# Another order at the beginning of six selective-scan runs: staggered halves, one ScalarE table, du's second half behind the first scan units

## The reference, cut to what matters

```
dbc = u @ W_xp                     # 64 + 16 + 16 columns
dt  = softplus(dbc[:64] @ W_dt + b_dt)
h_t = exp(dt_t * A) * h_(t-1) + (dt_t * u_t) * B_t
y_t = sum_s h_t[s] * C_t[s] + u_t * D
```

## Time and profile before

| | |
|---|---|
| median of 3 runs | 1971.57 us (1970.94 to 1975.65) |
| profiled execution | 1970.25 us |
| its span in the trace | 1968.5 us |
| TensorE matmul busy | 1868.5 us (95%) |
| VectorE busy | 1602.0 us (81%) |
| ScalarE busy | 1421.5 us (72%) |
| GpSimd busy | 1046.7 us (53%) |
| mean granted TensorE clock | 0.976 |

### The profile page before, as it was taken

How to read it: one execution, slowest core, us unless ns; L and a number is a source line. 1 busy time by engine, 2 the same in 40 slices (tenths; PEclk the granted TensorE clock), 3 DMA queues, 4 the chain that set the end, 5 groups by cost and what they waited for, 6 DMA issues and landing times. The chain is left out here.

```text
span 1968.5 us, 32685 instructions
## 1 busy us (share of the span) xinstructions
PE 1868.5 (95%) x12312; PEld 1344.0 (68%) x12312; DVE 1602.0 (81%) x2125; ACT 1421.5 (72%) x2666; POOL 1046.7 (53%) x603
## 2 busy tenths in 40 slices
PE   6989999999999999989999999989998999999997
PEld 3664899748997599869995799689974323332323
DVE  5665999668997699879995999689977989999742
ACT  3425999378992899699953999699944277777775
POOL 3031699417994299829980599469943500003000
PEclk9989899999999999999999999999999799999999
DMA  5022212102121112101110112021101111111000
GB/s 199 1 92 90 65 55 59 46 15 79 55 60 49 34 55 60 44 22 56 60 39 2 38 60 55 23 65 55 59 19 28 40 39 38 37 36 37 20 23 22
DMA packets 57548, 95.19 MB, mean 48 GB/s; under 512 B 14951, under 2 KB 23559, under 8 KB 55982
## 3 DMA queue, kind: packets, MB, share of 16 engines
q1 hardware_dynamic: 55854, 88.90, 15.2%
q0 software_dynamic: 1536, 4.20, 0.7%
HBM read 73.55 MB, written 6.91 MB: 41 GB/s over the span
## 5 line engine op out<-in xcount | busy, mean ns | idle before, releaser
L973 POOL TENSOR_TENSOR A<-A 128x1024 f32<-128x1024 f32 x384 | 895.8, 2409 | 231.9 <-ACT small L885 191.9
L893 ACT ACTIVATE A<-A,negA 128x512 f32<-128x512 f32 x768 | 549.1, 717 | 30.5 <-DVE A L954 23.7
L954 DVE TENSOR_TENSOR_SCAN A<-A,small,PS 128x512 f32<-128x512 f32 x384 | 453.8, 1257 | 8.2 <-ACT A L893 5.1
L954 DVE TENSOR_TENSOR_SCAN A<-A,PS 128x512 f32<-128x512 f32 x384 | 431.7, 1198 | 21.6 <-PE PS L806 10.9
L831 PE MATMUL PS<-ident,A 128*128 128x128 f32 x3072 | 401.9, 274 | 12.8 <-POOL A L973 9.4
L806 PE MATMUL PS<-A 128*128 128x128 f32 x3072 | 383.6, 276 | 0.3
L806 PEld LDWEIGHTS PS<-A 128*128 128x128 f32 x3072 | 362.4, 192 | 4.5 <-DVE A L954 1.3
L831 PEld LDWEIGHTS PS<-ident,A 128*128 128x128 f32 x3072 | 348.0, 141 | 20.0 <-POOL A L973 12.2
L1730 ACT ACTIVATE A<-PS 128x512 f32<-128x512 f32 x512 | 267.9, 603 | 123.6 <-PE PS L1693 123.4
L1499 DVE TENSOR_REDUCE A<-PS 128x1 f32<-128x512 f32 x512 | 319.7, 681 | 40.0 <-PE PS L1486 38.6
L870 ACT ACTIVATE A<-A,small 128x512 f32<-128x512 f32 x320 | 229.5, 717 | 14.1 <-PE PS L812 14.0
(11 more groups left out here) (194 smaller groups left out, 1837.9 us busy)
## 6 DMA issues: line engine op xcount, KB each, us to landing
A<-scrc SPq DMA_DIRECT2D x192, 256.0 KB, 3.2
A<-A SPq DMA_DIRECT2D x360, 32.0 KB
scr<-A SPq DMA_DIRECT2D x4, 1024.0 KB, 4.9
W<-in_wa SPq DMA_DIRECT2D x2, 1536.0 KB, 9.8
X<-in_x SPq DMA_DIRECT2D x4, 512.0 KB, 5.4
scr<-W SPq DMA_DIRECT2D x128, 1.5 KB
out<-X SPq DMA_DIRECT2D x4, 512.0 KB, 2.9
W<-in_w SPq DMA_DIRECT2D x1, 1984.0 KB, 7.6
```

The costliest lines, as they stand in the source:

```text
L893: e.activation(A_B[i % 4], r.DT[:, dt, ci * 512:(ci + 1) * 512], ACT.Exp, scale=negA[:, r.n, dt * 16 + s:dt * 16 + s + 1]).then_inc(*decay ...
L954: e.tensor_tensor_scan(h, a, u, init, ALU.mult, ALU.add).then_inc(*scanned.up((q, i)))
L973: e.tensor_tensor(h, h, CB[k % 2].unsqueeze(1).broadcast_to([128, 2, 512]), ALU.mult).then_inc(*weighed.up((q, pair)))
```

## The change

- **Halves staggered.** TensorE's order in a beginning becomes: xd of the first half, `more(0)`, dt of the first, xd of the second, `more(1)`, dt of the second, B turned, `more(2)`, du's first half turned, `more(3)`. ScalarE goes through Abs and Exp of the first half, the second's xd copy, `more(1)`, Abs of the second, B, Ln of the first, Exp and Ln of the second. `more` hands out the other work in parts: in runs 2 and 4 part 0 is the last 2 of this direction's 8 z projections and parts 1 to 3 are 1, 3 and 4 of the next direction's; in runs 3 and 5 part 0 is empty and parts 1 to 3 are 1, 3 and 4 of the gates; in runs 0 and 1 parts 0 and 1 are empty and the fused weights stand whole in part 2 on TensorE and in part 3 on ScalarE.
- **VectorE's other work** (`meanwhile`) moves between the two halves' du.
- **One table.** `preload_exp` goes; one `preload_act_table_set("natural_log_exp_and_others")` stands at the beginning. The gates' Silu is replaced by Identity with the bias, and a separate `open_gates_s` takes Silu in place, half by half, behind ScalarE's scan loop.
- **Next xd early.** Runs 3 and 5 get their first half's xd between the last sums of the run before (`early`, behind pair 61 of 64), and its copy behind ScalarE's loop.
- **du's second half later.** Its four turned blocks follow `form_u(3)` to `form_u(6)`; its copies stand at i = 3 and 4 of the loops of ScalarE and VectorE. All first scalings now stand ahead of the copies of the first half. `form_u(i)` for i < 4 waits for the copy of block i alone.

```diff
+        def turn_du_t(e, w, r, p, j):
+            o = take(w, ("dut", r.q, p, j))
+            w.wait_ge(*dve.at(("du", r.q, p)))
+            for m in range(4):
+                t = e.transpose(o[:, m * 128:(m + 1) * 128], DUD[:, p, m, j * 128:(j + 1) * 128], ident[:, :])
+            t.then_inc(*pe.up(("dut", r.q, p, j)))
...
+            if not begun:
+                banks.seek(4)
+                project_xd_t(e, w, r, r.order[0], ready)
+            more(0)
+            banks.seek(5)
+            project_dt_t(e, w, r, r.order[0])
+            project_xd_t(e, w, r, r.order[1], ready)
+            more(1)
+            banks.seek(3)
+            project_dt_t(e, w, r, r.order[1])
...
+            more(2)
+            banks.seek(4)
+            for j in range(4):
+                turn_du_t(e, w, r, 0, j)
+            more(3)
+            banks.seek(0)
...
+            if not begun:
+                copy_xd_s(e, w, r, r.order[0])
+            more(0)
+            e.preload_act_table_set("natural_log_exp_and_others")
+            size(0)
+            decline(0)
+            copy_xd_s(e, w, r, r.order[1])
+            more(1)
+            size(1)
...
+            log(0)
+            decline(1)
+            log(1)
+            more(2)
...
@@ run_t
                 form_u(i + 3)
+                if i < 4:
+                    turn_du_t(e, w, r, 1, i)
...
                 add_up(pair)
+                if pair == PAIRS_N - 3 and early:
+                    early()
...
@@ run_s
+            for j in range(4):
+                if not first_state(r, j)[2]:
+                    scale_du_s(e, w, r, j)
             for j in range(4):
                 if not first_state(r, j)[2]:
                     copy_du_s(e, w, r, 0, j)
-            if after:
-                after()
+            more(3)
+            w.wait_ge(*act.at(("bt", q, r.order[1])))
             for j in range(4):
                 spread_b(1, j)
-            for j in range(2, 4):
-                copy_du_s(e, w, r, 1, j)
             first_half(w, r)
...
                 if i >= 4:
                     decay(i)
+                if i in (3, 4):
+                    copy_du_s(e, w, r, 1, i - 1)
                 if dt % 2 and i >= 5:
                     keep((i - 5) // 2)
...
@@ run_v
+                if i in (3, 4):
+                    copy_du_v(e, w, r, 1, i - 3)
...
+        PARTS = (slice(0, 0), slice(0, 1), slice(1, 4), slice(4, 8))
...
+        def open_gates_s(e, w, b):
+            w.wait_ge(*act.at(("mx", b)))
+            for p, c in enumerate(runs[3 + 2 * b].order):
+                g = MX[:, :, c * 512:(c + 1) * 512]
+                e.activation(g, g, ACT.Silu).then_inc(*act.up(("gate", b, p)))
```

More of the change, by code:

```diff
@@ L656, in inputs_t @@
                 t.then_inc(*pe.up(("bt", q, c)))
[L657 to L667, removed]
@@ L677, in inputs_s, with copy_xd_s, size @@
+            more(3)
+            banks.seek(0)
+        def copy_xd_s(e, w, r, c):
+            w.wait_ge(*pe.at(("xd", r.q, c)))
+            e.activation(XD[0:96, c * 512:(c + 1) * 512], bank(("xd", r.q, c))[0:96, :], ACT.Copy).then_inc(*act.up(("xd", r.q, c)))
+            banks.give(("xd", r.q, c), act.now())
+        def inputs_s(e, w, r, more, begun=False):
+            q = r.q
+            def size(p):
                 for m in range(4):
-                    w.wait_ge(*pe.at(("dt", q, m, c)))
@@ L741, in inputs_v @@
                 e.tensor_tensor(DUD[:, p, :, :], r.DT[:, :, o], r.U[:, :, o], ALU.mult).then_inc(*dve.up(("du", q, p)))
-            if after:
-                after()
-            w.wait_ge(*act.at(("bt", q, r.order[0])))
+                if meanwhile and p == 0:
+                    meanwhile()
+            if late:
+                late()
+            for j in range(4):
+                if first_state(r, j)[2]:
+                    scale_du_v(e, w, r, j)
             for j in range(4):
@@ L747, in inputs_v @@
                     copy_du_v(e, w, r, 0, j)
-            for j in range(2):
-                copy_du_v(e, w, r, 1, j)
         def second_half(w, r):
@@ L899, in run_s @@
                 decay(i)
-            if meanwhile:
-                meanwhile()
+            for j in range(4):
+                if not first_state(r, j)[2]:
+                    scale_du_s(e, w, r, j)
             for j in range(4):
@@ L1197, in norm3_p, with z_jobs, z_t @@
             norm_p(e, w, ("ln3", b), range(b * TB, (b + 1) * TB))
-        def z_t(e, w, b, n):
+        PARTS = (slice(0, 0), slice(0, 1), slice(1, 4), slice(4, 8))
+        def z_jobs(n):
+            return [(m, c) for c in runs[2 + n].order for m in range(4)]
+        def z_t(e, w, b, n, jobs):
             w.wait_ge(*act.at(("wzc", n)))
-            for c in runs[2 + n].order:
-                for m in range(4):
-                    w.wait_ge(*act.at((("xs", b), c, 1)))
-                    project_t(e, w, ("z2", b, n, m, c), lambda k, m: Wzc[n][:, k, m * 128:(m + 1) * 128], 2, m, lambda k: XS[:, k, c * 512:(c + 1) * 512])
@@ L1206, in z_s @@
-        def z_s(e, w, b, n, halves=(0, 1)):
-            w.wait_ge(*dve.at(("bzc", n)))
-            for c in [runs[2 + n].order[p] for p in halves]:
-                for m in range(4):
-                    w.wait_ge(*pe.at(("z2", b, n, m, c)))
-                    e.activation(Z2[n][:, m, c * 512:(c + 1) * 512], bank(("z2", b, n, m, c)), ACT.Identity,
-                                 bias=Bzc[:, 4 * n + m:4 * n + m + 1]).then_inc(*act.up(("z2", b, n, c)))
-                    banks.give(("z2", b, n, m, c), act.now())
```

142 lines of the change are left out of this document (82 added, 60 removed).

## The result

The changed kernel takes 1979.66 us (median of 9 runs, 1978.34 to 1981.04), the kernel before 1973.65 in the same session (9 runs, 1970.23 to 1975.65). The ratio is 1.0034, interval 1.0023 to 1.0044: about 6.7 us slower by the ratio, 4.5 to 8.7 (the medians differ by 6.0). The forecast was +2.8. The direction holds, and so does the range of 1967 to 1983, which was wide; but the change costs more than twice what I worked out. It lies just beyond the 0.3% of a tie, and the interval does not settle on which side of 0.3% it is. A single execution of 5462.62 us in experiment 8 is left out of its median and ratio.

A forecast was written before the change was run, and what follows sets the result against it. GpSimd was taken to bound six scan runs (0 to 5), so only first weighings move: 2.6+2.2+1.3-4.3+1.3-0.3 = +2.8 us on 1971.57, giving 1974.4, range 1967 to 1983.

The forecast's parts named there:

- The first weighing sets the run: GpSimd has almost no gap inside a run, so each run ends 149 to 150 us after its first weighing with C.
- Rival 1: The first scan of each run decides, not the first weighing: -17 us, 1954.6; chance 0.06.
- Two ScalarE copies ahead of `keep(0)`, +1.0: ScalarE's copies of du's second half precede the first carry's saving at loop steps 3 and 4: +1.0 us in every run.
- Four steps of about 0.5, 2.1 in all: TensorE's form 4, turn 1, form 5, turn 2 make ScalarE wait +0.6 to 0.7 us; lower bound 0, upper 1.5.
- Rival 3: TensorE jams in the first units, forms and turned blocks interleaving at the low clock: +10 us, 1983; chance 0.16.
- The weight load, +2.2 and -0.3: In runs 1 and 5 SP's weight load waits for the last turned block, C loads behind it: first weighing +2.2, -0.3 us.
- Rival 4: The weight loads don't hold C back: run 5 gains 2.9 more, run 1 about 2.5, 1969; chance 0.10.
- Pace inside, 0: GpSimd's time inside each run stays at 149 us, so the insides of the runs add 0 us.
- my own sign of being wrong: The prediction would be wrong if GpSimd had gaps of its own inside a run, or the first carry preceded the copies.
- Table loads, 16 to about five, hidden in four starts: Eleven dropped loads, 14.1 us of ScalarE, count nothing in runs 0, 1, 2, 4, where TensorE is later.
- Rival 2: ScalarE's table loads were on the path: -14.1 us, 1957.5; chance 0.06.
- Early xd, -4.3 in run 3: The first half's xd fills TensorE's gap between the last sums, so run 3's first weighing comes at 869.9 against 874.28.

The follow-up runs named there:

- experiment 8: Changed kernel with du's second half ahead of the first unit, C ahead of the weight load in runs 0, 1, 5, carries two steps earlier: 1959.30 us.
- experiment 1: Changed kernel with ScalarE's two copies of du's second half moved behind the first carry, `keep(0)`: 1974.70 us, ratio 1.000 to the kernel before.
- experiment 2: Changed kernel with the first two C loads issued ahead of the weight load in runs 1 and 5: 1969.15 us, ratio 0.9978 to the kernel before.
- experiment 4: Changed kernel with ScalarE's copies behind `keep(0)` and, in runs 1 and 5, the first C loads ahead of the weight loads: 1961.01 us, ratio 0.9938.
- experiment 6: Kernel before with every carry saved two steps earlier in ScalarE's loop: 1970.17 us, ratio 0.9977.
- experiment 7: Changed kernel with ScalarE's copies behind the first carry, C ahead of the weight load in runs 0, 1, 5, carries two steps earlier: 1953.86 us.
- experiment 5: Kernel before with the first two C loads issued ahead of the weight load in runs 1 and 5: 1971.10 us, ratio 0.998.
- experiment 10: The kernel of experiment 4 with two more table loads in each beginning, ahead of the first Ln: 1982.69 us, ratio 1.0053 to the kernel before.
- experiment 9: The kernel of experiment 4 without the early xd in runs 3 and 5: 1968.99 us, ratio 0.998 to the kernel before.
- experiment 12: The kernel of experiment 11 with VectorE's other work moved between the halves of the maximum: 1953.84 us, ratio 0.9891 to the kernel before.
- experiment 11: The kernel of experiment 7 with the halves not staggered in runs 0 and 1: 1952.91 us, ratio 0.9902 to the kernel before.

## Why the prediction was off in size

- **The first weighing sets the run.** Right for the kernel before and the changed one, shown by the releasers and by experiments 1, 2 and 4. It stops being so when the weighing comes earlier (experiments 6 and 7). Rival 1 (the first scan decides) falls: counted from the end of the run before (838.77 and 830.10), run 3's first scan, at 871.48, is 6.8 earlier than in the earlier trace rows, but its weighing came only 2.8 earlier; in run 1 it is at 447.52, and the weighing 14 us later.
- **Two ScalarE copies ahead of `keep(0)`, +1.0.** Right: 0.49 each from start to start.
- **"Four steps of about 0.5, 2.1 in all", +0.6 to 0.7 of waiting.** This step failed. I took the four-matmul turned block of the earlier trace rows for the form as well. A form of an odd state is eight matmuls and takes 0.89; from the start of form 4 (873.75) to ScalarE's copy of block 2 (876.68) it is 2.93 instead of 2.1, and ScalarE waits 1.57. That is 0.9 more in each start that the carry decides, and experiment 1 takes the wait away with the copies (-2.4 to -2.8). It is my upper bound, "1.5 where the clock is low", reached with the clock at 1.00.
- **Rival 3** (TensorE jams in the first units) thus gave the right sign and place, and the wrong reason. In run 3 the clock is 1.00 over the first forms. In run 1 it was low (446.0 to 449.8 granted 0.54), but in experiment 2's profile the same forms ran at full clock and the last turned block was no earlier against run 0's end (90.1 us, in the changed kernel 89.1), since TensorE then waits for ScalarE.
- **The weight load, +2.2 and -0.3.** Mechanism right, size off by 2.0 and 2.1: it waits for the last turned block, which stands behind three forms and three blocks. From the start of the first block (449.65) to the start of what stands behind the last one (454.07) it is 4.4, where seven steps of 0.5 make 3.5. That is 0.9 of it. In run 1 form 0 also began 1.1 later than I had it (446.30, with 443.9 reckoned and the run before ending 1.3 later). Measured are +4.2 and +1.8, with the weighing 7.3 and 6.7 behind the issue, where 7.3 and 6.3 were reckoned. Rival 4 falls with experiments 2 and 5.
- **Pace inside, 0.** Failed, and by my own sign of being wrong, as GpSimd has gaps inside runs 1 and 5. It is +3.9 in this profile. 2.5 of it stand in runs 1 and 5, and the late C is a cause there: with C first they are 2.2 shorter. In run 1 it takes the low clock behind TensorE's wait as well (above).
- **Table loads, 16 to about five, hidden in four starts.** Half wrong. Eight are left: one in every beginning, where I expected the preload to be dropped when the set is already in, and two for Silu. Two more loads in a beginning are on the path in runs 2 to 5 (experiment 10), so my words that runs 2 and 4 hide them don't hold for the order of experiment 4. Rival 2 as I priced it falls all the same: no 14 us were gained. What the dropped loads gave in runs 2 and 4, against the later carry, is in the net of +1.6 and +0.1 (+1.6 at equal clock, see below); I have not separated it.

Groups of ScalarE's instructions by line (busy us, mean ns | idle before and its cause), table loads of the changed kernel:

```profile
L708 ACT ACT_TABLE_LOAD x6 | 7.7, 1283 | 0.5 <-DVE A L819 0.5
...
L1275 ACT ACT_TABLE_LOAD x2 | 2.6, 1283 | 0.0
```

- **Early xd, -4.3 in run 3 (my 869.9 against 874.28 is -4.4).** Right: -2.8 with the 0.9 more of the carry in it. Experiment 9 gives 8.0 for both runs, and in its profile 3.4 and 3.5 for the part alone once the clock is taken out.
- **Stagger, +1.5 in runs 0 and 1.** Right in run 0 by the profiles: two gaps of 0.7, and 1.4 less in experiment 12's. The times of experiments 11 and 7 don't separate it, and that it leaves the turned blocks at the low clock is not shown.
- **Silu behind the loop, 0.** Right as far as the sum of the insides and the tail (+0.3) shows; it was not tried by itself.

Run 4's start came out 1.5 better than run 2's, though both do the same. It is the clock at the very end of run 3, over the same 21 matmuls (L983, L195 and L265, now L1025, L195 and L265), before and after:

```profile
1028.80:1033.60 4.80, 4.80 (x21) 3.67 (x19) 4.47 (x11) 0.00 (x0) 0.00 (x0) 0.65 0.00 0
1035.20:1038.60 3.40, 3.40 (x21) 2.57 (x19) 3.40 (x8) 0.00 (x0) 0.00 (x0) 1.00 0.00 0
```

The low clock isn't a property of either kernel. Experiment 5's profile, an edit of the kernel before, has 1.00 there and a gap of 78.21 instead of 79.79. Experiment 2's, an edit of the changed kernel, has 0.65 and a gap of 81.50 instead of 79.92. So the +0.1 of run 4 is +1.6 at equal clock, against a forecast of +1.3.

Left open is how much of the 1.4 inside runs 0, 2, 3 and 4 has a cause and how much is chance.

## What to carry to other kernels

When a pipeline's slowest member never idles, ask only what its first element waits for, and put everything not needed for that element behind it on every engine and queue: here moving the carry and C was worth 19 us with no work removed (experiment 4). Count a moved step in the instructions that it is issued as, form by form, and not in "steps". And once the slow member starts earlier, look whether it is still the slowest: with starts 3 to 12 us earlier than in the changed kernel (experiment 7, 38.4 us in the six gaps), the runs took 10.5 longer inside, and over a quarter of the gain went back. And before you read a difference of 1 or 2 us off two profiles, compare the granted clock over the same instructions: here it moved gaps that no edit touched by 1.5 to 1.7 us.

## What the runs showed of the hardware

- A ScalarE load in front of TensorE cost more than itself: 2.6 us of loads became 4.2 to 4.4 at four starts, as TensorE's wait grew from 1.75 to 4.46 us and its granted clock was 0.52 to 0.58 over the following 16 matmuls (experiment 10).
- The same matmuls ran at either clock from one profile to the next, though no edit touched them: 21 of them took 4.80 us at 0.65 and 3.40 at 1.00, the last sum and xd 1.7 us more at 0.82 than at 1.00 (experiment 5 and the kernel before).
- The 256 KB loads of C queued behind one of 1,408 or 1,024 KB took a median of 6.8 or 6.0 us to land, and released GpSimd 7.3 or 6.7 us after the large one's issue (changed kernel), at a median of 3.2 for all in the kernel before.
- Preloading an activation table that is already in still costs its 1.28 us: in run 3 of the changed kernel the load stands at 842.22, though ScalarE had loaded no other table since the same load at 652.47.
